# The boundary of two experts at 128 tokens: 16 slots of 256 tokens and one of 128

## What is computed

```python
# x: (8, 512, 512) = 4096 tokens of 512; 16 heads; 2 experts with a hidden size of 2048
xn = _layernorm(x, axis=-1)
s = _L0_attn_ref(xn, Wqkv, b_qkv, Wout, b_out)      # causal attention with ALiBi
# the expert part, on x_flat = xn.reshape(4096, 512)
probs = jax.nn.softmax(x_flat @ w_router.T, axis=-1)
top_idx = jnp.argmax(probs, axis=-1)
top_weight = jnp.take_along_axis(probs, top_idx[:, None], axis=1)[:, 0]
h = jnp.einsum('nd,ehd->enh', x_flat, w_fc)
a = jnp.square(jnp.where(h >= 0, h, 0.5 * h))
expert_out = jnp.einsum('enh,edh->end', a, w_proj)
out = jnp.einsum('end,en->nd', expert_out, mask * top_weight[None, :])
x = x + s * _silu(out)
```

## Time and profile before

| | us |
|---|---|
| median of 3 runs | 1582.1 |
| their range | 1580.22 to 1586.92 |
| the profiled execution's own time | 1582.49 |
| its span, first to last instruction | 1579.8 |
| end of the attention block, DMA of `mall` issued | 803.3 |
| first matmul of slot 0 | 826.8 |
| last slot, from PE's last work for slot 15 to its own last matmul | 1524.7 to 1561.1 |
| last scatter handed over by POOL | 1569.2 |

### The profile page before, as it was taken

One profiled execution on the slowest core, in us unless ns is written; L12 is line 12 of the kernel. 1 busy time (PEld: TensorE's weight loads), 2 busy tenths in 40 slices (PEclk: granted clock), 3 DMA queues, 4 the chain that ended last, 5 costly groups with the idle time before them and its releaser, 6 DMA issues. The chain is left out here.

```text
span 1579.8 us, 32881 instructions
## 1 busy us (share of the span) xinstructions
PE 1426.5 (90%) x9912; PEld 902.2 (57%) x9912; DVE 940.1 (60%) x2432; ACT 774.1 (49%) x1826; POOL 691.5 (44%) x900
## 2 busy tenths in 40 slices
PE   2889999979999799999749999999999999999995
PEld 1455555645555355555426666666666666666663
DVE  7567776757667567776628954544444545545442
ACT  3477776757777567777606532222222222222221
POOL 0456556545555556556513443333333333333321
PEclk9999999989999899999969999999999999999998
DMA  4424334232533324333146611110111111111000
GB/s 150 155 86 135 101 116 140 88 116 88 158 98 101 114 87 145 101 114 122 41 131 218 202 41 33 32 32 28 41 41 39 30 41 41 41 41 42 17 21 31
DMA packets 85162, 134.24 MB, mean 85 GB/s; under 512 B 14207, under 2 KB 63359, under 8 KB 82816
## 3 DMA queue, kind: packets, MB, share of 16 engines
q1 hardware_dynamic: 75808, 105.70, 20.9%
q0 software_dynamic: 9184, 26.36, 5.3%
HBM read 98.34 MB, written 34.21 MB: 84 GB/s over the span
## 5 line engine op out<-in xcount | busy, mean ns | idle before, releaser
L1018 PE MATMUL psF<-xT,wf 128*128 128x256 f16 x3264 | 381.8, 274 | 6.7 <-DVE wf L1121 6.7
L1036 PE MATMUL psY<-wf,aT 128*128 x1632 | 374.3, 379 | 0.0
L1018 PEld LDWEIGHTS psF<-xT,wf 128*128 x3264 | 320.9, 98 | 74.2 <-issue 7.4
L1224 POOL TENSOR_TENSOR a<-a 128x512 f32<-128x512 f32 x136 | 156.7, 1152 | 410.3 <-DVE a L1138 408.8
L872 POOL TENSOR_SCALAR pr<-pr,rden 128x128 f32<-128x128 f32 (+3 forms) x512 | 269.5, 545 | 151.0 <-DVE rden L802 149.7
L562 ACT ACTIVATE pr<-pr,mn 128x128 f32<-128x128 f32 (+3 forms) x512 | 281.8, 553 | 0.0
L791 DVE CUSTOM_DVE_ANT_0 pr<-psS,base,nsl 128x128 f32<-128x128 f32 (+3 forms) x512 | 250.4, 544 | 16.9 <-issue 12.4
L1036 PEld LDWEIGHTS psY<-wf,aT 128*128 128x128 f16 x1632 | 159.8, 98 | 163.8 <-issue 0.2
L439 PE MATMUL psT<-conf,pr 128*128 128x128 f32 x1280 | 210.0, 283 | 37.7 <-POOL pr L872 23.7
L439 PEld LDWEIGHTS psT<-conf,pr 128*128 128x128 f32 x1280 | 160.6, 145 | 103.9 <-issue 36.5
L345 PE MATMUL psA<-xT,wqkv 128*128 128x512 f16 x768 | 196.4, 395 | 20.2 <-DVE wqkv L644 13.1
(11 more groups left out here) (137 smaller groups left out, 1385.5 us busy)
## 6 DMA issues: line engine op xcount, KB each, us to landing
qk_parts<-pre SPq DMA_DIRECT2D x64, 256.0 KB, 2.2
qs<-qk_parts SPq DMA_DIRECT2D x128, 128.0 KB, 2.6
ks<-qk_parts SPq DMA_DIRECT2D x128, 128.0 KB, 2.6
wst<-in_wf SPq DMA_DIRECT2D x16, 1024.0 KB
wstage<-in_wf SPq DMA_DIRECT2D x32, 512.0 KB, 4.6
xin<-in_x SPq DMA_DIRECT2D x32, 256.0 KB
attn_out<-so SPq DMA_DIRECT2D x32, 256.0 KB, 2.2
pt<-in_wqkv SPq DMA_DIRECT2D x4, 768.0 KB, 10.3
```

What stands on the lines that cost most here:

```text
L1018: last = nc.tensor.matmul(psF[c % 2][:, k * TT:(k + 1) * TT], w(e, 2 * hc, hl, kc * 512 + col, P), xT[:, r % 2, x, kc, :], start=(m == 0), ...
L1036: last = nc.tensor.matmul(psY[r % 2][h][:], aT[:, c % 4, x, k, h * P:(h + 1) * P], w(e, 2 * hc + 1, hl, q * 512, 512), start=(c == 0 and k ...
L1224: nc.gpsimd.tensor_tensor(at, at, at, ALU.mult).then_inc(s["a_ready"], 1)
```

## The change

The boundary is handled at 128 tokens instead of 256. All 4096 tokens make 32 tiles of 128, and the boundary tile of 128 is worked on twice, so there are 33: 16 slots of two and a last one of one. `halves(n)` tells how many halves slot n has, and every operation of the last slot, and of what prepares and finishes it, is done for one half: `up` streams 128 tokens instead of 256, with the same 24 matmuls and 16 addresses for a chunk; `down` has 6 matmuls instead of 12; the elementwise operations take two stretches of 128 columns instead of 512; there is one gather, one transposition, one tanh and one scatter instead of two.

The setup behind the attention block gets 17 operations where 5 stood. Bit 7 of `n0` tells which expert has an odd number of tiles of 128. That expert's single tile goes last; `tint` counts in tiles of 128. Since slot 0 may now belong to expert 1, `eint` tells whether a slot's expert differs from slot 0's, and `ebase` holds where the weights of the first and of the second expert in use begin. SP reads these two values into registers before its first weight load, and each of its 32 loads takes its address from one of them.

Of the diff, the parts that matter here (what is left out passes `ebase` on, and puts `halves` in place of `NH` in the other waits and loops of the same kind):

```diff
@@ -73,7 +73,7 @@
     for i in range(QB):
         c[:, C_TOK + i] = i * P + p
     c[:, C_NSL:C_NSL + H] = -slope[None, :]
-    c[:, C_SLOT:C_SLOT + SLOTS] = TT * np.arange(SLOTS)[None, :]
+    c[:, C_SLOT:C_SLOT + SLOTS] = TT * np.arange(SLOTS)[None, :] + P
     return c
 
 
...
@@ -844,12 +846,26 @@
             setup(nc.vector.tensor_tensor(x(X_CY), x(X_CY), x(X_PA2), ALU.mult))
             setup(ts(x(X_CY), x(X_CY), 2.0 ** -8, None, ALU.mult))
 
-            setup(ts(n0[:], esum[:, 0:1], -1.0, float(TOK), ALU.mult, ALU.add))
-            setup(ts(n0[:], n0[:], float(TOK - 1), None, ALU.min))
+            LAST = SLOTS - 1
+            setup(ts(n0[:, 0:1], esum[:, 0:1], -1.0, float(TOK), ALU.mult, ALU.add))
+            setup(ts(n0[:, 0:1], n0[:, 0:1], float(TOK - 1), None, ALU.min))
+            setup(nc.vector.tensor_copy(n0i[:, 0:1], n0[:, 0:1]))
+            setup(ts(n0i[:, 1:2], n0i[:, 0:1], P, None, ALU.bitwise_and))
+            setup(ts(n0i[:, 0:1], n0i[:, 0:1], TOK - P, None, ALU.bitwise_and))
+            setup(nc.vector.tensor_copy(n0[:, 1:3], n0i[:]))
+
             setup(ts(eslot[:], conf[:, C_SLOT:C_SLOT + SLOTS], n0[:, 0:1], None, ALU.is_gt))
-            setup(nc.vector.tensor_copy(eint[:], eslot[:]))
-            setup(nc.vector.scalar_tensor_tensor(out=tint[:], in0=conf[:, C_SLOT:C_SLOT + SLOTS], scalar=1.0 / TT,
-                                                in1=eslot[:], op0=ALU.mult, op1=ALU.subtract))
+            setup(ts(eslot[:, LAST:SLOTS], n0[:, 2:3], 1.0 / P, None, ALU.mult))
+            setup(ts(n0[:, 3:4], n0[:, 1:2], -1.0, float(TOK - P), ALU.mult, ALU.add))
+            setup(ts(tf[:], eslot[:], n0[:, 2:3], -1.0, ALU.mult, ALU.mult))
+            setup(nc.vector.tensor_tensor(tf[:], tf[:], conf[:, C_SLOT:C_SLOT + SLOTS], ALU.add))
+            setup(ts(tint[:], tf[:], 1.0 / P, -1.0, ALU.mult, ALU.add))
+            setup(ts(tf[:, 0:1], eslot[:, LAST:SLOTS], n0[:, 3:4], n0[:, 1:2], ALU.mult, ALU.add))
+            setup(ts(tint[:, LAST:SLOTS], tf[:, 0:1], 1.0 / P, None, ALU.mult))
+
+            setup(ts(eint[:], eslot[:], eslot[:, 0:1], None, ALU.not_equal))
+            setup(ts(ebase[:, 0:1], eslot[:, 0:1], 2.0 * HC, None, ALU.mult))
+            setup(ts(ebase[:, 1:2], eslot[:, 0:1], -2.0 * HC, 2.0 * HC, ALU.mult, ALU.add))
 
         @block.gpsimd
         def _(pool):
...
@@ -917,7 +933,12 @@
     return n + (c + lead) // GR, (c + lead) % GR
 
 
-def ffn_block(nc, io, sc, conf, mall, eslot, eint, tint):
+def halves(n):
+
+    return 1 if n == SLOTS - 1 else TT // P
+
+
+def ffn_block(nc, io, sc, conf, mall, eslot, eint, tint, ebase):
 
     with ExitStack() as ctx:
         sb = lambda n, s, d: ctx.enter_context(nc.sbuf_tensor(n, s, d))
...
@@ -977,11 +1002,13 @@
 
         @block.sync
         def _(sp):
+            stored_as = [sp.value_load(ebase[0:1, e:e + 1], min_val=0, max_val=NP) for e in range(E)]
             for k, n in enumerate(order):
                 if k >= RING:
                     sp.wait_ge(s["ws_lo"], k - RING + 1)
                 c = n % 2 * HP
-                sp.dma_start(wstage[:, k % RING, :], io["wf"][n // 2, :, c:c + HP]).then_inc(w_in[k % RING], 16)
+                sp.dma_start(wstage[:, k % RING, :], io["wf"][bass.ds(stored_as[n // 2 // NP] + n // 2 % NP, 1), :, c:c + HP]
+                             .rearrange("o p n -> (o p) n")).then_inc(w_in[k % RING], 16)
 
         @block.tensor
         def _(pe):
...
@@ -1005,18 +1032,19 @@
 
                 t, hc = n * GR + c, c // 2
                 if c == 0:
-                    wait(pe, s["X_lo"], (n + 1) * NH)
+                    wait(pe, s["X_lo"], n * NH + halves(n))
                 if n < PRE:
                     wait(pe, s["ws_lo"], arrival[4 * (n * HC + hc) + 1])
                 wait(pe, s["f_sum"], t - 1)
+                tn = halves(n) * P
                 for k in range(2):
                     col = (2 * (c % 2) + k) * P
                     m = 0
                     for hl, parts in ((0, (0, 1)), (1, (0,))):
                         for kc in range(KC):
                             for x in parts:
-                                last = nc.tensor.matmul(psF[c % 2][:, k * TT:(k + 1) * TT],
-                                                        w(e, 2 * hc, hl, kc * 512 + col, P), xT[:, r % 2, x, kc, :],
+                                last = nc.tensor.matmul(psF[c % 2][:, k * TT:k * TT + tn],
+                                                        w(e, 2 * hc, hl, kc * 512 + col, P), xT[:, r % 2, x, kc, 0:tn],
                                                         start=(m == 0), stop=(m == 3 * KC - 1))
                                 m += 1
                 last.then_inc(s["F_done"], 1)
...
@@ -1032,7 +1060,7 @@
                 for k in range(2):
                     q = 2 * (c % 2) + k
                     for m, (x, hl) in enumerate(((0, 0), (1, 0), (0, 1))):
-                        for h in range(NH):
+                        for h in range(halves(n)):
                             last = nc.tensor.matmul(psY[r % 2][h][:], aT[:, c % 4, x, k, h * P:(h + 1) * P],
                                                     w(e, 2 * hc + 1, hl, q * 512, 512),
                                                     start=(c == 0 and k == 0 and m == 0),
...
@@ -1135,15 +1163,16 @@
                 wait(dve, s["f_relu"], t + 1)
                 wait(dve, s["U_lo"], t - 1)
                 wait(dve, s["U_hi"], t - 1)
-                nc.vector.scalar_tensor_tensor(out=a[:, c % 2, :], in0=psF[c % 2][:], scalar=2.0 ** -28,
-                                               in1=rl[:, c % 2, :], op0=ALU.mult, op1=ALU.add
+                nc.vector.scalar_tensor_tensor(out=part(a[:, c % 2, :], n), in0=part(psF[c % 2][:], n),
+                                               scalar=2.0 ** -28, in1=part(rl[:, c % 2, :], n),
+                                               op0=ALU.mult, op1=ALU.add
                                                ).then_inc(s["f_sum"], 1)
 
             def alo(n, c):
                 t = n * GR + c
                 wait(dve, s["U_hi"], t + 1)
-                tt(aT[:, c % 4, 1, :, :].rearrange("p k n -> p (k n)"), a[:, c % 2, :],
-                   aT[:, c % 4, 0, :, :].rearrange("p k n -> p (k n)"), ALU.subtract).then_inc(s["U_lo"], 1)
+                tn = halves(n) * P
+                tt(aT[:, c % 4, 1, :, 0:tn], part(a[:, c % 2, :], n), aT[:, c % 4, 0, :, 0:tn], ALU.subtract).then_inc(s["U_lo"], 1)
 
             def step(n, r):
                 done = within(n - 1, 0, SLOTS)
...
@@ -1220,10 +1249,10 @@
                     nu, cu = ahead_of(n, c, LEAD)
                     if within(nu, 0, SLOTS):
                         wait(pool, s["f_sum"], nu * GR + cu + 1, s["apart_pool"])
-                        at = a[:, cu % 2, :]
+                        at = part(a[:, cu % 2, :], nu)
                         nc.gpsimd.tensor_tensor(at, at, at, ALU.mult).then_inc(s["a_ready"], 1)
                     if c == 1 and within(n - 1, 0, SLOTS):
-                        for h in range(NH):
+                        for h in range(halves(n - 1)):
                             wait(pool, s["o_ready"], (n - 1) * NH + h + 1, s["apart_pool"])
                             nc.gpsimd.indirect_dma_start(
                                 out=io["out"], out_offset=bass.IndirectOffsetOnAxis(ap=oidx[:, h:h + 1], axis=0),
```

61 lines of the change are left out of this document (33 added, 28 removed).

## The result

| | before | after |
|---|---|---|
| median, us | 1583.9 (4 runs) | 1557.99 (4 runs) |
| range, us | 1580.22 to 1586.92 | 1556.27 to 1562.05 |
| the profiled execution | 1582.49 | 1562.05 |
| its span | 1579.8 | 1560.2 |

The ratio is 0.9841, with an interval of 0.9811 to 0.9872. The kernel is faster by 1.6% (1.3 to 1.9%). The forecast was 1558.6 us in a range of 1555.5 to 1564.5.

What follows compares the result with a forecast made beforehand. PE's own work was taken to bound the steady slots. PE's work -21.05, stalls +0.8, end -2.8, setup +0.3 and gather -0.8 sum to -23.55 us: 1558.9 from the profiled 1582.49, 1558.6 against the median, range 1555.5 to 1564.5.

Steps and rivals of the forecast that it cites:

- PE's work in the last slots: Last slot and two `up` chunks in slot 15: shorter `up`, halved `down`, one transposition less save 21.05 us.
- Rival A: Last slot's `up`: weight loads don't hide at 128 columns, 5.4 us more, 1564.0 us; chance 0.10.
- C: Last slot: `up` doesn't get shorter, something fixed takes 109 ns per matmul; 10.25 us back, 1568.9 us; chance 0.03.
- B: Last slot: PE's sequencer becomes the bound at 150 ns per address instruction; 2.9 us more, 1561.5 us; chance 0.08.
- E: Weight loads with a register in their address land much later, making the kernel slower: 1590 us and above; chance 0.02.
- The stalls: Last slot: PE waits for work that doesn't halve, at chunk 3's `down` and behind the last `up`; 0.8 us.
- The end: Behind the last matmul: one scaling, one product and the second scatter go, saving 2.8 us.
- The setup: Gap between the blocks: twelve more operations, mostly covered by the landing of `mall`; 0.3 us stick out.
- The register loads: Gap between the blocks: SP's two loads delay the first weights from 807.9 to about 809.8, covered by loads of `x`.
- with weights 2 us later less of them is ahead: Gap between the blocks: slot 0's second gather lands sooner in the DMA engines, a gain of 0.8 us.
- Rival D: Gap between the blocks: the gather gets the DMA engines to itself, 2.3 us more gain, 1556.3 us; chance 0.05.
- the gap term: Gap between the blocks: setup +0.3 and the gather's gain -0.8, together -0.5 us.

Runs made afterwards that it cites:

- e3: Kernel after, with `up` of the last slot streaming all 256 columns again; 1571.23 us, ratio 0.9923.
- e7: Kernel after, with 24 instead of 16 address instructions for each `up` chunk of the last slot, same matmuls; 1572.61 us in one execution.
- e4: Kernel after, with twelve more one-element operations at the end of the setup chain; 1563.17 us in one execution.
- e1: Kernel after, with fixed addresses for the weight loads again, without SP's two register loads; 1559.77 us, ratio 0.9857.
- e2: Kernel after, with SP holding all weight loads back until both gathers of slot 0 have landed; 1557.46 us, ratio 0.9831.
- e9: Kernel before, with the early weight split and the held weight loads of e6; 1571.94 us, ratio 0.995.
- e6: e5 with weight loads from the third piece on held back until both gathers of slot 0 have landed; 1552.27 us, ratio 0.9807.
- e0: Kernel after, unchanged, run again for a tighter interval and a second profile; 1560.83 us, ratio 0.9859.
- e5: Kernel after, with the first two pieces of weights split before slot 0's normalisation and the next splits moved up; 1553.64 us, ratio 0.9823.

## Why the prediction held, step by step

**PE's work in the last slots: right.** Predicted 21.05 us saved, with 0.8 of stalls back: 20.25. Measured: slot 16 is 17.34 shorter and slot 15 is 2.99 shorter: 20.33 together. Of the 2.99, two short `up` chunks make 2.56 (e3 gives just that back: 42.12), and the 0.43 left fits the transposition's 0.44. The prediction gave slot 15 the steady slot's 42.84 us, where it has 42.55, but its terms came from the rows of the single chunks and don't hang on that. e3 gives the width of `up` alone 9.7 us.

**Rival A** (weight loads show at 128 columns) is refuted by the 1.34 us of 24 matmuls, and **C** by the same row and e3. The Trainium skill (TensorE: Matmul & The Clock Gate, section Back-to-back issue gap) has about 81 ns at 128 columns for such a stream; the trace doesn't agree, with 55.8 ns over 24 in a row. **B** wasn't at work, since the pair is 2.63 us as its matmuls alone would make it, but e7 shows that the pace of 125 ns, and with it the thin cover of 5%, was read rightly. **E** is refuted by the time and by the weight loads' median from issue to landing, 4.8 us against 4.6.

**The stalls: right in size, wrong in place.** Predicted 0.8, of it 0.6 at `down` of chunk 3 for want of a low part that stands behind the finish of slot 15 on DVE. There is none there: DVE's low part begins at 1533.56 and ends at 1533.98, and PE comes to it at 1534.67. DVE was quicker than costed, with 1.70 for the two products instead of 2.13 and 0.98 for the last operation instead of 1.41. What stalled PE, as I read the trace, was POOL; no run moved the scatters to test it. Its two scatters of slot 15 (1533.03 to 1535.74) stand ahead of the square of chunk 4, which starts only at 1535.74, and `down` of chunk 4 starts 0.12 late at 1537.43. From there the squares start 1.93 to 1.96 us apart, each behind the relu and sum of its chunk, and the last `down` waits 0.5 us for the last low part. Of the 36.44 us before, six short `up` (7.68 saved) and eight short `down` (10.36 saved) leave 18.40; the measured 19.10 makes 0.70 of stalls. The prediction named POOL's two scatters nowhere in that chain, though their order on POOL's queue stands in the program.

**The end: right.** Predicted -2.8, measured -2.87.

**The setup: right.** Predicted +0.3 us for what of the twelve operations sticks out behind the landing of `mall`, measured +0.32 at the second gather. e4 shows that the cover is gone: twelve more cost 2.25 us.

**The register loads: right as a delay, wrong in what follows.** The first weights leave 1.85 us later, where 1.9 was predicted; 1.54 of it is SP's register loads (e1) and the rest the setup. ACT finds them landed when it wants them, as predicted. But the step "with weights 2 us later less of them is ahead" failed: it counted -0.8, and the wait for the gather grew by 1.1. The prediction saw the DMA engines as a line in which the gather gets through sooner if less was issued ahead of it. The runs say otherwise. With the weights leaving at 4.65 to 4.97 the wait is 6.6 to 6.7 (before, e1). With 6.50 it is 7.6 to 8.7 (both profiles of after, e3, e7), and with weights and gather both 2.25 later 8.9 (e4). With no weights about it is 3.52 (e2). The same direction shows with half of the weights and slot 1's gathers out of the way: the second gather lands in 3.8 us when the weights left 3.1 us ahead of it (e9), and in 5.0 when they left 1.55 ahead (e6).

The packets' records tell how. The first packet of a gather starts 4.1 us behind the first gather's issue in after and 4.6 in before, against 1.9 in e2. By then 0.87 MB of the 2.1 MB of weights have moved in after, and 1.52 in before (0.88 in e0, 1.52 in e1). From there both kinds move side by side: in after 1.26 MB of weights and 1.04 MB of gathers between 816.5 and 823.5. So weights that leave earlier have moved more of their bytes before the gathers' data begin, and have fewer left to share with. The wait has two parts: the late first packet (some 2.2 us in after, 2.7 in before) and the sharing (4.3 - 2.2, some 2 us in after, 0.4 in before). It is the second that grew. Rival D, with the gather alone, is thereby no case of this kernel: e2 had to hold the weights back for it.

**What the sum missed.** It counted -0.5 for the gap. Measured is +1.44 at the first matmul, of which 0.32 is the setup and 1.1 the wait; in slot 0 about half is taken back, and at its end +0.73 is left (+0.92 in e0). The 0.35 in slot 8 and the -0.24 behind the last scatter stand in no term. All in all the sum gave 23.55 us from `mall` on and the traces have 22.38 and 22.21, so it took 1.2 us too much, and the gap term alone is wrong by that (0.73 + 0.5). The stalls with PE's work, the end and the setup came out within 0.1 us each. That the medians came out at 1557.99 and 1560.83, around the forecast of 1558.6, is in part luck: they lie 25.9 and 23.7 us below those of the kernel before, more than the traces give the change. The difference is within what the attention part scatters by, though only one execution of each set was profiled.

**Open**: why the attention part ends anywhere from 801.8 to 810.4 us after the start for nearly the same code. It is the largest part of the scatter between executions, and no run here was made to explain it. Also open: what holds a gather's first packet back for over 2 us while weights move, what slot 0 takes back, and slot 8's 0.35 us. That a gather's data then share the engines is read from the packets and agrees with e1, e2, e6 and e9; no run changed the share itself.

## What to carry to other kernels

Where one engine is busy for a whole steady slot, work taken from it counts in full, and the row durations gave it to within 1% here (20.33 measured, 20.25 predicted): most of the care belongs to the two ends. When the chunks of a slot get shorter, go through every queue, scatters included, and ask which instructions that don't shrink now stand ahead of the next chunk's. And look at what stands in the pipeline's fill: the split of the weights in the wrong place cost 6 us at the end of slot 0 in the kernel after (e5), and with the held loads it is 7.7 to 8.0 us in both kernels (e6, e9), more than the register loads, the setup and the stalls together.
